# First attention: TensorE turns the maxima ahead of the next tile's scores, VectorE norms the next tile ahead of its copy of the turned queries

## The reference

```python
x = x + tanh(g_xattn[0]) * L0_xattn(layernorm(x), ctx_1024, ctx_1024)

# L0_xattn(q, k, v): 16 heads of 16 channels, no projections
scores = einsum('bqnd,bknd->bnqk', qh, kh) * scale
probs  = softmax(scores, axis=-1)
out    = einsum('bnqk,bknd->bqnd', probs, vh)

# then, not touched: a ternary-weight FFN with a convolution, a second
# attention with projections, and a mixture of 8 experts
```

## Time and profile before

| | |
|---|---|
| median of the 3 runs | 1871.5 us (1868.78 to 1871.53) |
| profiled execution | 1864.52 us, its span 1862.8 us |
| mean granted TensorE clock | 0.974 |
| busy share of the span | PE 85%, DVE 83%, ACT 64%, POOL 46% |
| first attention, about | 48 to 378 us of the span |

### The profile page before, as it was taken

The page is one execution under the profiler, slowest core; times in us unless marked ns, Lnnn a source line. Parts: engine busy times, 40 slices in busy tenths (PEclk is TensorE's granted clock), DMA queues, the critical chain, the costliest instruction groups (busy, mean ns, idle before and its releaser), DMA issues. The chain is left out here.

```text
span 1862.8 us, 47835 instructions
## 1 busy us (share of the span) xinstructions
PE 1574.3 (85%) x19034; PEld 1061.2 (57%) x19034; DVE 1552.0 (83%) x2913; ACT 1188.2 (64%) x1916; POOL 861.8 (46%) x929
## 2 busy tenths in 40 slices
PE   0799999846666666748999999995899999999998
PEld 0577777624444444435666666664566566665665
DVE  7699999847988888876999999996888888888885
ACT  1799999878788887726888888886233332333332
POOL 1455555427777877743333333331233333333332
PEclk9999999979999999969999999998899999999999
DMA  9200000000000000000000000000211211212211
GB/s 313 95 3 3 3 3 2 3 1 1 1 1 1 1 1 1 1 18 2 3 3 3 3 23 23 23 12 2 92 69 58 103 69 58 102 69 79 93 58 69
DMA packets 47886, 68.26 MB, mean 37 GB/s; under 512 B 8640, under 2 KB 39104, under 8 KB 47680
## 3 DMA queue, kind: packets, MB, share of 16 engines
q1 hardware_dynamic: 45312, 65.30, 10.3%
q10 hardware_dynamic: 2368, 0.02, 0.1%
HBM read 56.39 MB, written 8.65 MB: 35 GB/s over the span
## 5 line engine op out<-in xcount | busy, mean ns | idle before, releaser
L757 ACT ACTIVATE a_exp<-a_score_t 128x1024 f32<-128x1024 f32 x256 | 262.2, 1024 | 70.1 <-PE a_score_t L556 37.0
L1590 POOL TENSOR_TENSOR e_a_parts<-e_act,e_a_parts 128x512 f16<-128x512 f32 x128 | 153.3, 1198 | 329.2 <-ACT e_a_parts L1561 329.2
L1561 ACT ACTIVATE e_a_parts<-e_act 128x512 f16<-128x512 f32 x128 | 80.6, 630 | 303.9 <-DVE e_act L1393 272.3
L1137 POOL TENSOR_TENSOR b_hidden<-b_hidden,b_shifted 128x508 f32<-128x508 f32 x128 | 161.6, 1263 | 113.3 <-DVE b_hidden L987 113.3
L1275 PE MATMUL e_up_ps<-e_n_turned,e_up_t 128*128 128x512 f16 x768 | 187.9, 381 | 8.5 <-DVE e_act L1389 8.5
L1289 PE MATMUL e_out<-e_down_t,e_a_parts 128*128 128x256 f16 x1536 | 188.4, 273 | 0.8 <-POOL e_a_parts L1590 0.8
L1275 PE MATMUL e_gate<-e_n_turned,e_gate_t 128*128 128x512 f16 x768 | 187.9, 381 | 0.2 <-issue 0.2
L1289 PEld LDWEIGHTS e_out<-e_down_t,e_a_parts 128*128 128x128 f16 x1536 | 149.6, 98 | 39.0 <-POOL e_a_parts L1590 1.1
L1144 POOL TENSOR_TENSOR b_hidden<-b_hidden,b_scales 128x512 f32<-128x512 f32 x128 | 168.1, 1318 | 2.3 <-ACT b_scales L1119 2.3
L822 POOL TENSOR_TENSOR a_split<-ctx,a_split 128x256 f16<-128x256 f32 x64 | 42.9, 670 | 271.4 <-ACT a_split L776 271.4
L918 PE MATMUL b_hid<-b_x_turned,w1t 128*128 128x512 f16 x512 | 136.0, 390 | 26.6 <-DVE b_hidden L987 23.3
(11 more groups left out here) (207 smaller groups left out, 4011.9 us busy)
## 6 DMA issues: line engine op xcount, KB each, us to landing
ctx<-e_weights SPq DMA_DIRECT2D x64, 512.0 KB, 5.5
out<-x SPq DMA_DIRECT2D x16, 512.0 KB, 2.9
x<-in_x SPq DMA_DIRECT2D x3, 2048.0 KB, 19.0
ctx<-in_ctx SPq DMA_DIRECT2D x1, 4096.0 KB, 27.0
ctx<-in_ctx SPq DMA_DIRECT2D x1, 3072.0 KB, 16.5
a_exp<-in_L_ffn_w SPq DMA_DIRECT2D x2, 1024.0 KB, 9.6
a_q_turned<-a_neg_max_t SPq DMA_DIRECT2D x128, 2.0 KB
x<-in_x SPq DMA_DIRECT2D x1, 1536.0 KB, 16.4
```

The source lines that it names most:

```text
L757: nc.scalar.activation(exp32[:, u % 2, 2 * p:2 * p + 2, :], score_t[:, :].rearrange("p (g n) -> p g n", g=2), ACT.Exp, scale=DH ** -0.5 / ...
L1137: nc.gpsimd.tensor_tensor(dst, dst, shifted[:, c % 2, :].rearrange("p (t k) -> p t k", k=P)[:, :, 0:P - 1], ALU.add).then_inc(conv_ok, 1)
L1590: nc.gpsimd.tensor_tensor(a_parts[:, e % 4, 1, :], act3[:, e % 2, :], a_parts[:, e % 4, 0, :], ALU.subtract).then_inc(alo_ok, 1)
```

## The change

In layer 0 alone, TensorE issues `turn_maxima` ahead of `do_scores` pass 0 instead of behind it. A wait for `q_copied` is put in front, since the maxima are turned into the bank that held the turned queries; `do_scores` waits for the same count already. VectorE issues the norm of tile i ahead of the copy of the turned queries of tile i-1 instead of behind it. No instruction that computes is added or removed; layer 1 keeps its order.

```diff
@@ TensorE, step
                     uT, uS, uE, uV = ((u - lag) % UNROLL for lag in (TL, SL, EL, VL))
+                    if run_exps and not layer:
+                        reach(pe, q_copied, min(i - TL, TILES))
+                        turn_maxima(i - EL, uE)
                     if run_scores:
                         do_scores(i - SL, uS, 0)
-                    if run_exps:
-                        if layer and inside(i - 2, TILES):
+                    if run_exps and layer:
+                        if inside(i - 2, TILES):
                             reach(pe, ql_ok, i - 1)
                         turn_maxima(i - EL, uE)
@@ VectorE, step
                     if not layer and inside(i - STATS, TILES):
                         take_stats(i - STATS)
-                    if run_turn:
-                        reach(dve, q_turn, i - (TL - 1))
-                        nc.vector.tensor_copy(q_turned[...], q_bank[...]).then_inc(q_copied, 1)
                     if not layer and run_front:
                         reach(dve, qh_ok, i - 1)
                         reach(dve, ql_ok, i - 1)
                         nc.vector.tensor_scalar(normed[...], m.x[:, i, :], ...).then_inc(nf_ok, 1)
+                    if run_turn:
+                        reach(dve, q_turn, i - (TL - 1))
+                        nc.vector.tensor_copy(q_turned[...], q_bank[...]).then_inc(q_copied, 1)
                     if layer and run_fin:
                         divide(i - FL, uF)
```

More of the change, by code:

```diff
@@ L714, in step @@
                         take_stats(i - STATS)
-                    if run_turn:
-                        reach(dve, q_turn, i - (TL - 1))
-                        nc.vector.tensor_copy(q_turned[:, uT % 4, :, :], q_bank[:, :].rearrange("p (n k) -> p n k", k=P)).then_inc(q_copied, 1)
                     if not layer and run_front:
@@ L722, in step @@
                                                 ALU.subtract, ALU.mult).then_inc(nf_ok, 1)
+                    if run_turn:
+                        reach(dve, q_turn, i - (TL - 1))
+                        nc.vector.tensor_copy(q_turned[:, uT % 4, :, :], q_bank[:, :].rearrange("p (n k) -> p n k", k=P)).then_inc(q_copied, 1)
                     if layer and run_fin:
```

## The result

The changed kernel takes 1843.99 us (median of 4 runs, 1841.28 to 1844.27), the kernel before 1871.01 us (4 runs, 1868.78 to 1871.53): ratio 0.9855, 95% interval 0.9838 to 0.9872, so 27 us or 1.45% faster. The forecast was 1848 us in a range of 1842 to 1858. In two later comparisons the same changed kernel came out at ratios of 0.9860 (0.9835 to 0.9886) and 0.9850 (0.9831 to 0.9870).

The account below looks back on a forecast made before the run. TensorE's ring of 4.83 us a period was taken to bound the first attention. 56 x (4.835 - 4.50) = 18.8 us plus 4.6 at the start gave 23.4 off 1871.5: 1848 us, range 1842 to 1858.

Parts of the forecast that it names:

- TensorE's own ring: First attention: VectorE copies maxima, TensorE does its step's work and turns the next maxima; 4.83 us, setting the period.
- the 0.15 us of signalling: Time taken from the second maximum's end on VectorE to TensorE's turn, leaving that turn 0.14 us of slack.
- The turn's place: Maxima turned ahead of the scores on TensorE: 0.33 to 0.35 us saved a period; VectorE's first maximum 0.17 later.
- M: Start of VectorE's copy of the turned maxima, once a period; M' is the next one.
- The norm's place: Norm ahead of the queries' copy on VectorE: worth 0.12 us a period with the turn moved, nothing steady alone.
- The collision: Rival: VectorE's norm meets GpSimd's addition to x, missed by 0.02 us, and takes 0.44 longer; 1863 us, chance 0.07.
- the rule: VectorE in two-port mode and GpSimd hold a shared port pair exclusively, whoever starts first for its whole instruction.
- The average period: Steady period of the first attention after the change: 4.50 us instead of 4.835, over 56 periods, saving 18.8 us.
- the near ties: Thin slacks in the new period, for which a little was added to TensorE's 4.48 us to make 4.50.
- The start: First six periods and the time ahead of the first M: 4.6 us saved, between 2.3 and 6.6.
- The slower rival: Norm's wait for the queries' low part, slack 0.7 us, holds back the queries' copy on VectorE; 1881 us, chance 0.03.
- The whole: Sum of savings, 23.4 us: profiled execution from 1864.5 to 1841.1 us, median from 1871.5 to 1848.1.

Follow-up runs that it names:

- the kernel with the norm first: Changed kernel with VectorE's norm put right behind the copy of the turned maxima: 1856.63 us, 0.9945 of the kernel before.
- the two kernels with the norm first: Changed kernel with the norm right behind the maxima's copy, with the loop of eight steps (1856.63 us) and with steps written out (1838.66 us).
- the kernel with the early keys: Changed kernel, steps written out, TensorE turning three of eight key blocks between pass 0's scores and transposed scores: 1850.14 us, 0.9895 of before.

## Why the prediction was right, point by point

**The bound.** "TensorE's own ring sets the pace" is shown: the norm's move alone gave 0.02 us a period, the missing shift matmuls gave 0.14 in the new order, the missing statistics nothing. A detail was off. I took 4.83 for TensorE's ring; it is 4.81, as in rows 2's last period and in the kernel with the norm's move alone. In both the second maximum ends some 0.3 us earlier than in a steady period of before, so the other 0.02 belong to its being late there; how they arise is not shown. Nor do the runs bear out the 0.15 us of signalling that I put between a maximum and TensorE: where the scores really waited, they started 0.06 us behind its end (308.95 to 309.01 in the kernel with the norm first).

**The turn's place.** M' = M + 4.48 was forecast and 4.48 measured; scores 0.14 behind the turn, measured 0.16; first maximum at M + 0.31, measured 0.33 (300.85 to 301.18). The added wait for the queries' copy cost nothing.

**The norm's place.** Without it the period was forecast at 4.62, measured 4.61 to 4.62. Its worth of 0.12 to 0.14 a period is shown. The forecast of nothing in the steady part for the norm alone holds but for the 0.02.

**The collision.** It did not come: the norm takes 0.40 us (0.397 median, 0.449 longest of 64), and in the period shown it starts at 302.66, just as GpSimd's addition to x ends (301.94 + 0.72 = 302.66). The miss of 0.02 us was forecast and is 0.00 in this step. That the collision's price is real is shown in the two kernels with the norm first, 0.47 and 0.6 us for a period. The kernel without statistics shows that an overlap costs only from about 0.25 us on, as I had it: there the norm starts at 307.15, 0.32 us before the addition to x ends (306.74 + 0.73 = 307.47), and takes 0.47. The Trainium skill ("SBUF — State Buffer", section "Who interferes with whom") says that whichever of the two issues first has the shared pair for its whole instruction and the other is blocked. The traces agree that one is held to the other's end, the norm to 307.83 against 307.67. But by the starts shown the norm at 306.95 was held by an operation that began at 307.00, and so it is in rows 8, of which I had said that they agree with the rule: when the shown starts are this close, they don't decide which of the two is held.

**The average period** was taken as 4.50 and is 4.498, for the wrong reason, so this agreement is luck: I put 0.02 on the near ties, and the plain period has none of it. The loop of eight steps costs 0.14 + 0.05 once in eight, 0.024 on average. In the kernel before, in which VectorE waited for 0.25 us and more in each period, it showed as 0.01 to 0.02.

**The start** was mis-sized. I took 4.6 us up to the 7th copy, with 6.6 as the highest; measured 7.3. The first M is 1.5 us earlier (59.66 to 58.16), the next six periods save 5.8. TensorE's granted clock may have a part in it. These are two stretches of the kernel before, columns as in rows 1:

```profile
64.00:68.00 4.00, 2.37 (x38) 2.06 (x39) 2.52 (x4) 2.63 (x4) 0.67 (x1) 0.86 0.00 0
68.00:72.00 4.00, 3.69 (x71) 2.79 (x68) 2.65 (x5) 3.30 (x5) 1.62 (x3) 0.72 0.02 4
```

Means of 0.86 and 0.72 make 3.4 us at half clock (1.2 instead of 2.4 GHz), behind a stretch in which TensorE had waited for much of the time (from 64 to 66 us it was busy for 0.56 of 2, the clock still at 1.00). In the profiled execution after, the clock stays at 1.00 there, and so it does in the two kernels with one move each, whose 7th copies come at 90.07 and 88.51. What the half clock cost was not isolated, and there is one profile of the kernel before. In the third profile of the changed kernel the second copy comes 5.20 us after the first instead of 4.16, and the 7th at 85.72, with the clock at 1.00: 1 us of the 7.3 changes from execution to execution.

**The slower rival** was built on a wrong tile. The low part of the queries that ends at M + 0.74 in rows 5 is that of tile i-1; the norm of tile i waits for tile i-2, whose low part ended a period earlier. Its slack is then some 5 us and not 0.7, and the rival was still less likely than the 0.03 given.

**The whole.** 23.4 us were summed for the profiled execution and its span fell by 23.2; that is 26.1 of the stage less 2.9 of spread behind it. The medians are 27 apart, nearer to the stage's own gain. 1848 was high by 4 us: 2.7 for the start, the rest spread.

## What to carry to other kernels

When several engines are all busy for about nine tenths of the time, add up one period start to start round each ring, and test the sum where the trace itself leaves an operation out (here the last period, without a norm). Of two consumers behind one wait, issue first the one whose answer another engine must send back, and let the other fill the flight. A second move that is worth little alone can be worth several times as much once the first has been made (here 7.4 us instead of 1.3 in the steady part). So price both in the new order too, with the loop's own turning and each changeover of tile form among the costs. Before work is moved into a gap, follow the chain that starts behind the gap: in the kernel with the early keys it ran over ScalarE and back.

## What the runs showed of the hardware

- A VectorE tensor_scalar on fp32 in SBUF (the norm, 0.40 us alone) that is shown to start up to 0.09 us ahead of a GpSimd operation, or while one runs, ends no earlier than about 0.15 us after that operation's end: 0.88, 0.82 and 0.84 us in the rows shown, 0.91 with the longest such lead (278.22 against 278.31, norm first), 0.47 without the statistics. In all 13 profiles 188 norms met an operation in this way, and none ended earlier than 0.12 us after it. With 0.11 us of lead it isn't held (301.11 against 301.22), and the GpSimd operation is the longer one (0.82 instead of 0.67).
- A norm whose column is addressed by a loop register carries 93 and 40 ns of register instructions on VectorE's sequencer. Behind a short copy of 0.22 us it started 0.16 us later than without them; the loop itself went with them, so they are the likely cause and not a shown one.
- TensorE's change from 64-row tiles to 128-row tiles and back takes about 0.1 us each way (0.33 instead of 0.22, 0.27 instead of 0.17, early keys).
- Turning the loop of eight steps cost VectorE 0.15 us in a steady step of the changed kernel (its copy 0.42 us behind the turn instead of 0.27).
